# Splitting the gate and up weights of each expert block into two rounded parts, in an MoE stage on one core

## The reference, cut to what matters

```
top_logits, top_idx = jax.lax.top_k(x_flat @ Wr.T, 2)
hg = jnp.einsum('eih,th->eti', Wg, x_flat)      # 256 -> 512
hu = jnp.einsum('eih,th->eti', Wu, x_flat)
y = jnp.einsum('ehi,eti->eth', Wd, jax.nn.silu(hg) * hu)   # 512 -> 256
return jnp.einsum('eth,te->th', y, cw)
```

## Time and profile before

| | us |
|---|---|
| median of 3 runs | 768.18 |
| lowest and highest | 766.91, 771.41 |
| the profiled execution, device time | 766.19 |
| the profiled execution, span first to last instruction | 764.4 |
| TensorE busy | 601.8 (79%) |
| VectorE busy | 479.9 (63%) |
| ScalarE busy | 276.2 (36%) |
| GpSimd busy | 263.1 (34%) |

### The profile page before, as it was taken

How to read it: one execution, slowest core, us unless ns; L and a number is a source line. 1 busy time by engine, 2 the same in 40 slices (tenths; PEclk the granted TensorE clock), 3 DMA queues, 4 the chain that set the end, 5 groups by cost and what they waited for, 6 DMA issues and landing times.

```text
span 764.4 us, 10605 instructions
## 1 busy us (share of the span) xinstructions
PE 601.8 (79%) x3606; PEld 399.8 (52%) x3606; DVE 479.9 (63%) x1060; ACT 276.2 (36%) x535; POOL 263.1 (34%) x242
## 2 busy tenths in 40 slices
PE   3933667877676869999459998888878799999991
PEld 2721335655552758888225555455445456666660
DVE  6869997969768765695497777877774211221223
ACT  1376433223110212345207664554435432222220
POOL 3157467745265743447572001001016011111111
PEclk9975669989867999999659999999999999999996
DMA  6101200000011200168995663260003892000005
GB/s 186 53 27 55 79 2 0 1 1 0 0 39 42 74 10 1 55 122 161 193 266 78 85 85 50 37 84 2 3 15 115 332 421 87 21 21 28 22 21 178
DMA packets 43619, 58.35 MB, mean 76 GB/s; under 512 B 7184, under 2 KB 37072, under 8 KB 42544
## 3 DMA queue, kind: packets, MB, share of 16 engines
q1 hardware_dynamic: 41696, 52.55, 28.9%
q0 software_dynamic: 1872, 5.13, 1.9%
HBM read 41.97 MB, written 15.51 MB: 75 GB/s over the span
## 4 chain that ended last, share of the span: by engine, by line
PE 38%; DVE 10%; DMA 3%; issue 2%; ACT 2%; POOL 1%; SPq 0%; POOLq 0%; DVEq 0%; ACTq 0%
PE bank L745 19%; DVE small L1679 4%; PE bank L992 4%; PE bank L969 4%; PE bank L942 4%; PE bank L739 4%; DMA pieces<-P 2%; PE bank L944 1%; PE bank L971 1%; POOL P L2094 1%; DVE mtok L1690 1%; PE bank L1009 1%; DMA yt<-results 1%; ACT PTa L1265 1%; DVE XA L1708 0%
## 5 line engine op out<-in xcount | busy, mean ns | idle before, releaser
L1679 DVE TENSOR_REDUCE small<-bank 128x1 f32<-128x256 f32 (+3 forms) x256 | 107.3, 482 | 9.1 <-PE bank L944 8.1
L745 PE MATMUL bank<-wall,xt 128*128 x184 | 82.8, 593 | 0.0
L1999 POOL TENSOR_TENSOR al<-hm,ah 128x512 fp32r<-128x512 f32 (+1 forms) x28 | 40.9, 1462 | 91.4 <-ACT ah L1228 91.4
L942 PE MATMUL bank<-Ks,Qs 96*128 96x256 bf16 (+3 forms) x256 | 67.2, 330 | 5.3 <-DVE small L1679 3.7
L1938 DVE TENSOR_TENSOR bhm<-bsg,bank 128x512 f32<-128x512 f32 x23 | 15.8, 687 | 83.9 <-PE bank L745 83.9
L969 PE MATMUL bank<-Qs,Ks 99*128 99x512 bf16 (+3 forms) x256 | 58.8, 306 | 5.0 <-issue 4.6
L944 PE MATMUL bank<-maskb,identb 128*128 128x128 bf16 x256 | 55.6, 236 | 0.0
L1550 DVE TENSOR_TENSOR_SCAN S<-AT,U 128x512 f32<-128x512 f32 x32 | 49.7, 1554 | 8.2 <-POOL QS L2017 7.9
L1265 ACT ACTIVATE PTa<-bank 128x512 f32<-128x512 f32 (+1 forms) x96 | 43.6, 528 | 29.5 <-PE bank L971 29.2
L1265 ACT ACTIVATE PTb<-bank 128x512 f32<-128x512 f32 (+1 forms) x96 | 43.7, 529 | 28.9 <-PE bank L971 28.5
L745 PEld LDWEIGHTS bank<-wall,xt 128*128 128x128 f32 x184 | 33.2, 190 | 33.0 <-issue 33.0
(11 more groups left out here) (344 smaller groups left out, 1513.6 us busy)
## 6 DMA issues: line engine op xcount, KB each, us to landing
wall<-e_pack SPq DMA_DIRECT2D x8, 1536.0 KB, 15.2
pieces<-P SPq DMA_DIRECT2D x12, 512.0 KB, 9.9
Qs<-pieces SPq DMA_DIRECT2D x48, 128.0 KB, 5.4
Ks<-pieces SPq DMA_DIRECT2D x48, 128.0 KB, 6.0
stg<-w_pack SPq DMA_DIRECT2D x18, 256.0 KB, 2.7
wf<-t_pack SPq DMA_DIRECT2D x12, 256.0 KB, 2.6
sorted_rows<-blank SPq DMA_DIRECT2D x1, 2944.0 KB, 13.9
yt<-results SPq DMA_DIRECT2D x8, 256.0 KB, 4.7
```

The source lines that it names most:

```text
L745: last = nc.tensor.matmul(outap, a, b_, start=start and i == 0, stop=stop and i == n - 1, **kw)
L942: nc.tensor.matmul(banks[b][:, o:o + w], Q[0:96, h, i * P:(i + 1) * P], K[0:96, h, 0:w], start=True, stop=False)
L1679: last = nc.vector.tensor_reduce(mxv[:, i, h:h + 1], banks[b][:, o:o + w], AX.X, ALU.max, negate=True)
L1999: nc.gpsimd.tensor_tensor(al[0:M, s % 3, :], hm[0:M, s % 3, :], ah[0:M, s % 3, :].bitcast(F32), ALU.subtract).then_inc(*alr.tick(s))
```

## The change

Gate and up become split products: six MATMULs per half instead of two float32 products. `xt` becomes `xh` and `xl`. ScalarE copies each half of the block's weights (128 x 1024 floats) from its place in `wall` into `wh`, rounding it; VectorE subtracts that from `wall` into `wl`. Both engines now read the place of the block into a register of their own. This work for block i+1 stands around `gu(i)` in the programs. The down product stays as it was.

For room, the three parts of the sorted rows lie elsewhere: blocks 0 to 7 in `rows`, 8 to 18 in `xga`, 19 to 22 in `xgc`; `wh`, `wl` and `xgc` lie over the old `XTh`, `XTl`, `X1h` buffers, and parts 1 and 2 are loaded after all experts' weights.

```diff
-XG_PARTS = [(0, XGA), (XGA, XGA + NC * CH // P), (XGA + NC * CH // P, BLOCKS)]
+XG_PARTS = [(0, NC * CH // P), (NC * CH // P, NC * CH // P + XGA), (NC * CH // P + XGA, BLOCKS)]
...
-        ORDER.append(("bx", 0))
+        ORDER += [("bx", 0), ("bw", 0, 0), ("bw", 0, 1)]
         for i in range(BLOCKS):
             if i + 1 < BLOCKS:
-                ORDER.append(("bx", i + 1))
+                ORDER += [("bx", i + 1), ("bw", i + 1, 0)]
             ORDER.append(("gu", i))
+            if i + 1 < BLOCKS:
+                ORDER.append(("bw", i + 1, 1))
             if i >= 1:
                 ORDER.append(("dn", i - 1))
             ORDER.append(("ht", i))
...
-            sp.wait_ge(*w_split.upto(len(JOBS) - 1))
             for j in range(2):
                 sp.wait_ge(s_put[j], 16 * NT)
             sorted_part(0)
             for k in range(2, EARLY):
                 expert_weights(k)
-            sorted_part(1)
             for k in range(EARLY, NE):
                 expert_weights(k)
+            sp.wait_ge(*w_split.upto(len(JOBS) - 1))
             sp.wait_ge(*mm.upto(("wout", 3, 1)))
+            sorted_part(1)
             sorted_part(2)
...
-                claim(6, bxh, i)
+                claim(6, bxl, i)
...
-                pe.wait_ge(s_wb[min(i, NE - 1)], 16)
                 for half, who in ((0, bgate), (1, bhid)):
                     b = 2 * half + i % 2
                     claim(b, who, i)
-                    product(banks[b][:], [(xt[:, k], wall[:, bass.ds(w0 + (half * KC + k) * EI, EI)]) for k in range(KC)])\
-                        .then_inc(*mm.tick(("gu", i, half)))
+                    pe.wait_ge(*wsl.upto((i, half)))
+                    wh, wl = moe["wh"][:, i % 2, half], moe["wl"][:, i % 2, half]
+                    terms = []
+                    for k in range(KC):
+                        terms += [(xh[:, k], wh[:, k]), (xl[:, k], wh[:, k]), (xh[:, k], wl[:, k])]
+                    product(banks[b][:], terms).then_inc(*mm.tick(("gu", i, half)))
...
+                elif op == "bw":
+
+                    _, i, half = it
+                    if half == 0:
+                        if i == 0:
+                            act.wait_ge(*placed.upto("owner"))
+                            for pr in range(2):
+                                act.wait_ge(*mm.upto(("wout", 3, pr)))
+                        place = act.value_load(L1["place_i"][0:1, i:i + 1], min_val=0, max_val=(NE - 1) * EW)
+                        act.wait_ge(s_wb[min(i, NE - 1)], 16)
+                    if i >= 2:
+                        act.wait_ge(*mm.upto(("gu", i - 2, half)))
+                    nc.scalar.copy(flat(moe["wh"][:, i % 2, half]), wall[:, bass.ds(place + half * KC * EI, KC * EI)])\
+                        .then_inc(*wsh.tick((i, half)))
...
+                elif op == "bx":
...
+                    nc.vector.tensor_tensor(moe["xl"][:, i % 2], banks[6][:, 0:D].rearrange("p (k n) -> p k n", k=KC),
+                                            moe["xh"][:, i % 2].bitcast(F32), ALU.subtract).then_inc(*bxl.tick(i))
+                elif op == "bw":
...
+                        place = dve.value_load(L1["place_i"][0:1, i:i + 1], min_val=0, max_val=(NE - 1) * EW)
+                        dve.wait_ge(s_wb[min(i, NE - 1)], 16)
+                    dve.wait_ge(*wsh.upto((i, half)))
+                    nc.vector.tensor_tensor(flat(moe["wl"][:, i % 2, half]), wall[:, bass.ds(place + half * KC * EI, KC * EI)],
+                                            flat(moe["wh"][:, i % 2, half]).bitcast(F32), ALU.subtract).then_inc(*wsl.tick((i, half)))
```

More of the change, by code:

```diff
@@ L226, in build @@
         moe, _ = plan([("wall", [NE * EW], F32)], region + 4608)
-        m, o = plan([("xga", [XGA, ROW], F32)], x1_at + 10240)
+        m, _ = plan([("xga", [XGA, ROW], F32)], region + 103424)
+        moe.update(m)
+        m, o = plan([("bsg", [2, EI], F32), ("bhm", [2, EI], F32), ("hT", [2, EI], F32), ("xh", [2, KC, P], F32R),
+                      ("xl", [2, KC, P], F32R)], mlp_at)
+        assert o <= mlp_at + 20480
+        moe.update(m)
+        m, o = plan([("wh", [2, 2, KC, EI], F32R), ("wl", [2, 2, KC, EI], F32R), ("xgc", [BLOCKS - XGA - NT, ROW], F32)], xt_at)
         assert o <= mlp_at
         moe.update(m)
[L230 to L236, removed]
+        m, _ = plan([("yt", [2, NT, D], F32)], region + 4608)
         moe.update(m)
@@ L242, in block_rows_of @@
         def block_rows_of(i):
-            if i < XGA:
-                return moe["xga"][:, i, :]
+            if i < NT:
+                return rows[:, i, :]
             if i < XGA + NT:
-                return rows[:, i - XGA, :]
+                return moe["xga"][:, i - NT, :]
             return moe["xgc"][:, i - XGA - NT, :]
@@ L343, in build @@
         share_set = tally("row_shares_set")
-        bxh = tally("block_rows_turned")
+        wsh = tally("block_weights_high")
+        wsl = tally("block_weights_low")
+        bxh = tally("block_rows_high")
+        bxl = tally("block_rows_low")
         bgate = tally("block_gate")
@@ L690, in sorted_part @@
                 src = sorted_rows[b0 * P:b1 * P, :].rearrange("(b p) d -> p b d", p=P)
-                dst = (moe["xga"][:], rows[:], moe["xgc"][:])[j]
+                dst = (rows[:], moe["xga"][:], moe["xgc"][:])[j]
                 sp.dma_start(dst, src).then_inc(s_xg[j], 16)
@@ L1365, in _ @@
                         act.wait_ge(*mm.upto(("gu", i - 2, 1)))
[L1366 removed]
+                    nc.scalar.copy(moe["xh"][:, i % 2], banks[6][:, 0:D].rearrange("p (k n) -> p k n", k=KC)).then_inc(*bxh.tick(i))
+                elif op == "bw":
[11 more added lines that the diff above has]
+                        .then_inc(*wsh.tick((i, half)))
                 elif op == "gu":
@@ L1939, in _ @@
                         .then_inc(*bhid.tick(i))
+                elif op == "bx":
+                    i = it[1]
+                    dve.wait_ge(*bxh.upto(i))
+                    if i >= 2:
+                        dve.wait_ge(*mm.upto(("gu", i - 2, 1)))
+                    nc.vector.tensor_tensor(moe["xl"][:, i % 2], banks[6][:, 0:D].rearrange("p (k n) -> p k n", k=KC),
+                                            moe["xh"][:, i % 2].bitcast(F32), ALU.subtract).then_inc(*bxl.tick(i))
+                elif op == "bw":
+                    _, i, half = it
+                    if half == 0:
+                        if i == 0:
+                            dve.wait_ge(*placed.upto("owner"))
+                        place = dve.value_load(L1["place_i"][0:1, i:i + 1], min_val=0, max_val=(NE - 1) * EW)
[3 more added lines that the diff above has]
+                                            flat(moe["wh"][:, i % 2, half]).bitcast(F32), ALU.subtract).then_inc(*wsl.tick((i, half)))
                 elif op == "dn":
```

7 lines of the change are left out of this document (3 added, 4 removed).

## The result

| | before | changed | ratio |
|---|---|---|---|
| median of 4 runs each, us | 767.77 | 756.06 | 0.9831 [0.9805, 0.9857] |
| lowest and highest, us | 766.91, 771.41 | 753.0, 757.95 | |
| profiled execution, us (its span) | 766.19 (764.4) | 756.01 (754.2) | |

The changed kernel is 11.7 us faster; 757.5 was forecast. The profiled execution, which the sum of the terms was made for, gave 756.01 against a forecast of 755.5.

What follows compares the result with a forecast made beforehand. TensorE was taken to bound the block stage before and after. -12.8 us from gate and up plus 2.1 at the beginning gave -10.7: 755.5 for the profiled execution, 757.5 for the median, range 753.5 to 768.

Steps and rivals of the forecast that it cites:

- TensorE bounds the stage before and after: Block stage: wholly TensorE's before; its new block of 5.24 us stays longer than the other engines' loop of 4.88 us.
- The gain per block: Gate and up on TensorE: 3.44 us becomes 2.86, saving 0.58 per block, 12.8 us over 22 stretches.
- The total: Whole kernel: -12.8 + 2.1 = -10.7 us, so 755.5 for the profiled execution and 757.5 for the median.
- The figure of the page: Gate-and-up matmuls: 216 ns gap from the skill page instead of the trace's 232; the stretch would be 17.0 us shorter.
- The work beside it: ScalarE and VectorE copies, subtracts and offset reads per block: a 4.88 us loop, hidden with 0.36 us to spare.
- The beginning: First blocks have no earlier block to hide behind: turn of block 0 at 618.15 against 616.08, cost +2.1 us.
- Transfers: Loads of weights and sorted rows: all there before needed, counted zero; one late part would cost a few us.
- The clock falls at the beginning: Rival: TensorE nearly idle from 610.9 to 613.95, then 1.2 GHz for a stretch; +1.7 us, 759.2; chance 0.14.
- The offset reads are slow: Rival: ScalarE and VectorE register loads make the loop 5.76 us; 769.9, like no change; chance 0.12.
- The subtract at its long price: Rival: VectorE's subtract takes 2.166 us instead of 1.23 in every block and both halves; 783 us; chance 0.08.

Runs made afterwards that it cites:

- the kernel with two products: Changed kernel with the third product (`xh` by `wl`) left out of gate and up, the subtract still run and waited for: 748.29 us, 0.972.
- the added 0.69: Changed kernel plus a 512-column VectorE addition from block 1 on: ahead of the first half's subtract 774.0 us, 0.9945; ahead of the second's 766.85 us, 0.9843.
- the changed kernel's later run: Changed kernel unedited, run again on another chip beside the version with block 0 in float32: 768.35 us, 0.9874 to the kernel before.

## Why the prediction was right, point by point

**TensorE bounds the stage before and after.** Right: 30.00 of 30 us in both windows, and turns without a wait of their own.

**The gain per block.** Predicted 0.58, measured 5.82 - 5.15 = 0.67. Gate and up came out nearly as said (2.86 predicted, 2.84 measured, the second half without another 0.08). The term was mis-sized at the step from `bx` to gate and up, which the prediction let stand ("`dn`, `bx` and turn stay"): the float32 product started 0.22 us after the start of the `bx` pair (645.66 to 645.88), the fp32r one 0.14 after (656.54 to 656.68). This 0.08 and the 0.02 of gate and up are 0.09 a block after rounding, and 22 x 0.09 are the 2.0 us between -12.8 and -14.76.

**The total.** The forecast for the profiled execution was 755.5 us, and 756.01 was measured. So close a hit is luck. Inside the stage the forecast was -10.7 and the measured change -12.65 (133.45 to 120.80), 2.0 us more. Against that stood +1.83 ahead of the stage and +0.6 behind it, for which the prediction had no term.

**The figure of the page.** Matmuls of gate and up follow each other at 0.23 us (657.22 is 0.23 after 656.99), as in the earlier trace rows. The stretch got 14.8 shorter, but that is no test of the figure, since 2.0 of it come from another step; the pitch is. The 216 ns of the Trainium skill ("TensorE: Matmul & The Clock Gate", Back-to-back issue gap) aren't reached in this form of product.

**The work beside it.** `wh` was put at 1.04 and took 1.05, `wl` at 1.23 and took 1.22, and `xl` stayed below its 0.48 at 0.42. The offset was put at 0.7 from the start of the copy ahead, and is 0.43 in the steady state and 0.93 in block 0. The loop was 4.88 by the sum and 4.74 measured in the kernel with two products. The 0.27 too much for the offset was partly made up elsewhere: `wl` starts 1.25 us after the start of `wh` there, where 1.04 was put. That this loop is the next bound is shown by that kernel, whose turns wait for `bhm`, and by the added 0.69, which costs 0.32 a block inside the loop and 0.3 us in all outside.

**The beginning.** Predicted +2.1, measured +2.11. The steps were less exact than the sum: gate and up of block 0 started 3.97 after the first `bx` (3.50 predicted). The offset accounts for 0.19 of that (0.93 from `xh` to `wh`, 0.74 in the prediction); most of the rest lies between the start of `wh` and that of `wl`, 1.25 for some 1.05. That the sum held is luck too, because a second error lay against it: the read for block 1 was hidden (615.53 to 615.79, 0.26 against 0.7), so silu was done 0.5 earlier than I had put, and `bhm` of block 0 waited for the second half of gate and up, not for silu.

**Transfers.** Predicted 0, and the kernel with the places alone shows it: stage 133.47 against 133.46.

**The rivals.** *The clock falls at the beginning* (0.14) did not happen in the profiled execution that the result was read from, nor in the kernels with two products and with fixed offsets. It did in all five profiled executions of kernels with a split block 0 on the two slower chips: turn 0 came 9.3 us after the first `bx` in place of 7.7, +1.6 (forecast +1.7). It was sized rightly, and its chance of 0.14 was too small for those chips. *The offset reads are slow* (0.12): not so, 113.04 without them and 113.06 with them. *The subtract at its long price* (0.08): a GpSimd sum produced it, a DMA_INDIRECT does not. The prediction had put its border at 1.9 us with both halves stretched; with only the first half at 2.85 the period was already 6.37, above the 5.82 of the kernel before.

The rule of the Trainium skill ("SBUF — State Buffer", Who interferes with whom), that VectorE with two SBUF inputs contends with a GpSimd instruction that reads SBUF, as an exclusive lock, agrees with these runs and with the 1.09 us above; `bhm`, whose one input is a bank, kept its 0.68 beside the sum (680.55), as that section says of one SBUF input. The statement of the Trainium skill ("SBUF — State Buffer", SBUF: two separate sides) that whoever starts first gets the shared pair of ports for the whole instruction and the other fully blocks fits the blocks at 680.73, 645.36 and 269.12, but not the starts in the profile at 682.41: VectorE started 0.48 us before GpSimd and still was the one that waited. GpSimd's times in the profile are rough, and at 269.12 a lead of 0.22 us was enough for VectorE, so which of the two goes first can't be told from the recorded starts; that it is all or nothing can.

**What stays open.** No run tells why two of the chips take 9 us or more longer (the kernel before 778.7 and 778.3 us; first `bx` at 621 to 623 in every trace from them, 610 to 616 in the others), or what decides in an execution whether the clock falls after block 0's wait: in the profiled execution of the result TensorE had the same wait and the clock stayed, as its windows show:

```profile
612.60:616.00 3.40, 0.47 (x3) 0.20 (x2) 2.04 (x3) 2.74 (x5) 0.00 (x0) 1.00 0.98 412
616.20:619.60 3.40, 2.98 (x12) 2.18 (x12) 2.83 (x4) 3.37 (x4) 0.00 (x0) 1.00 1.03 434
```

TensorE's 0.47 us here answer to the 0.50 of the changed kernel's later run, and 1.00 stands where 0.54 stood. Between chips the two cases fell apart cleanly, none of three against five of five, but nothing was run to tell the chip from what happens ahead of the stage on it.

## What to carry to other kernels

When a change trades time of the busiest engine for work on others, add up no busy shares: write down the loop that returns to the busiest engine (here turn, `hT`, `xh`, `wh`, `wl`, `bhm`, turn), compare its length with that engine's period, and put every added instruction either in it or outside it. To measure a loop that is hidden, take work from the engine above it until the loop shows; adding a known piece inside and outside confirms it. And a preparation that runs one round ahead has no round to hide behind at the first: consider leaving the first round as it was. Here that, with the earlier table load, was worth 0.7%: 2.1 us for the beginning itself, and 1.6 us for a fall of the clock behind the idle stretch, which not every execution has.

## What was not expected of the hardware

- A VectorE subtract of two operands in the on-chip memory was stretched from 1.22 to 2.85 us by a GpSimd sum of 1.28 us that started 0.48 us after it, and to 1.92 by one that started 0.42 before it. In both cases, and in all 43 like them, it ended 1.08 to 1.10 us after the sum. Once, with the sum 0.77 us later, it was the sum that grew, from 1.28 to 1.58.
- A DMA_INDIRECT of 1.00 us wholly inside the same subtract made it 1.28 or 1.29 us long, 0.07 more at most.
- A register load on ScalarE cost less than its own length in the steady state: loads of 275 ns put `wh` 0.43 after the start of `xh`, 0.17 more than no load does. In block 0, behind an idle stretch, it was 0.67 more.
- In blocks 8 and 17 the step from `xh` to `wh` was 0.71 or 0.72 in all seven kernels that split block 0 and read the offset, and nowhere else. It was not there with fixed offsets, nor in the version with block 0 in float32, which has other instructions ahead of it. The loads themselves were no longer than the others (276 to 285 ns between 650 and 700 us). The cause is open. Where the loop had less than 0.28 us to spare it showed in the period (5.02 for 4.74, 5.75 for 5.47).
- The same program had its first `bx` at 610.45 in one execution and at 615.54 in another. From 560 us on the second has a granted clock of 0.51 from 570 to 577 and 0.52 from 611.0 to 614.4, the first 0.51 from 568.6 to 572.0 alone: what lies ahead of a stage can move by more than the 2 us of a term.
